# One scan of a state-space step moves behind the gating of the first expert slot

## The reference, cut to what matters

```python
ph   = exp(-(pr*pr + pi*pi)) * exp(1j * arctan2(pi, pr))
conv = ifft(fft(ph**n * pinit) * fft(x))           # along the 32 positions
h    = h + (conv + last * ph**n * ph).real         # the state-space layer
...
top_w, top_i = top_k(xf @ Wg, 2)                   # two of eight experts
y = silu(xf @ W1[e]) * (xf @ W2[e])                # gating: one product
h = h + sum over the two experts of  weight * (y @ W3[e])
```

## Time and profile before

| | |
|---|---|
| median of 3 runs | 538.47 us (538.28 to 539.43) |
| the profiled execution | 540.12 us, of which the span is 538.1 us |
| PE busy | 433.2 us, 81% of the span |
| DVE busy | 303.9 us, 56% |
| ACT busy | 199.4 us, 37% |
| POOL busy | 162.2 us, 30% |
| PE's clock, mean over the span | 0.91 of full speed |

### The profile page before, as it was taken

How to read it: one execution, slowest core, us unless ns; L and a number is a source line. 1 busy time by engine, 2 the same in 40 slices (tenths; PEclk the granted TensorE clock), 3 DMA queues, 4 the chain that set the end, 5 groups by cost and what they waited for, 6 DMA issues and landing times.

```text
span 538.1 us, 9170 instructions
## 1 busy us (share of the span) xinstructions
PE 433.2 (81%) x3291; PEld 282.7 (53%) x3292; DVE 303.9 (56%) x869; ACT 199.4 (37%) x369; POOL 162.2 (30%) x140
## 2 busy tenths in 40 slices
PE   0698798888657754737759999999799999999991
PEld 0254455555554543536525766676565666566561
DVE  0596958784699899998897577726431111111110
ACT  0244545254357513113422662254323233223321
POOL 6041010010020023531042546353254343454422
PEclk9999998979977957855679999999999999999997
DMA  9999010072054100543010422243123226232311
GB/s 179 245 211 204 13 32 3 25 248 84 15 164 179 34 13 2 177 153 132 10 40 11 118 39 41 40 118 50 27 43 49 50 39 185 49 58 39 48 22 19
DMA packets 36102, 43.14 MB, mean 80 GB/s; under 512 B 5216, under 2 KB 30560, under 8 KB 35904
## 3 DMA queue, kind: packets, MB, share of 16 engines
q1 hardware_dynamic: 26384, 32.14, 21.5%
q0 software_dynamic: 7488, 10.23, 12.1%
q10 hardware_dynamic: 2192, 0.27, 0.5%
HBM read 30.96 MB, written 11.53 MB: 79 GB/s over the span
## 4 chain that ended last, share of the span: by engine, by line
PE 57%; DVE 23%; DMA 7%; issue 7%; ACT 3%; SPq 1%; POOL 0%; POOLq 0%; DVEq 0%; ACTq 0%
PE psum L2026 22%; PE psum L2045 11%; PE psum L1723 8%; DMA KT<-in_L_attn_w_o_dram 3%; PE psum L2036 3%; PE psum L1736 2%; PE psum L1748 2%; DMA out_dram<-mixture_rows_out 2%; PE psum L1761 2%; PE psum L2016 1%; DVE st_att L998 1%; DMA KT<-mixture_rows_in,src_i 1%; DVE mx L1032 1%; PE psum L1852 1%; DVE O L1194 1%
## 5 line engine op out<-in xcount | busy, mean ns | idle before, releaser
L1625 DVE TENSOR_TENSOR QT<-QT,psum 128x512 f32<-128x512 f32 x39 | 26.8, 688 | 134.6 <-PE psum L2026 134.4
L1723 PE MATMUL psum<-M2s,M1s 128*128 128x512 f32 x128 | 60.3, 627 | 21.3 <-DMA M1s<-in_L_tok_W_dram 18.8
L2026 PE MATMUL psum<-M1s,KT 128*128 x156 | 75.5, 607 | 1.4 <-ACT KT L789 1.0
L2045 PE MATMUL psum<-M3s,KT 128*128 x312 | 74.2, 381 | 1.5 <-ACT KT L797 0.8
L2026 PE MATMUL psum<-M2s,KT 128*128 x156 | 73.3, 592 | 0.0
L2045 PEld LDWEIGHTS psum<-M3s,KT 128*128 128x128 f32 x312 | 58.5, 190 | 22.0 <-issue 15.9
L808 ACT ACTIVATE O<-psum,gate_slot 128x256 f32<-128x256 f32 x39 | 18.5, 474 | 108.8 <-PE psum L2045 106.0
L502 POOL DMA_INDIRECT KT<-mixture_rows_in,src_i x39 | 41.0, 1052 | 44.2 <-issue 23.3
L1723 PEld LDWEIGHTS psum<-M2s,M1s 128*128 128x128 f32 x128 | 25.1, 201 | 50.6 <-issue 30.0
L2026 PEld LDWEIGHTS psum<-M2s,KT 128*128 128x128 f32 x156 | 29.8, 191 | 37.6 <-issue 37.6
L529 POOL DMA_INDIRECT mixture_rows_out<-O,src_i x17 | 31.6, 1860 | 31.3 <-ACT O L808 12.5
(11 more groups left out here) (398 smaller groups left out, 732.6 us busy)
## 6 DMA issues: line engine op xcount, KB each, us to landing
M3s<-in_x_dram SPq DMA_DIRECT2D x4, 1024.0 KB, 10.6
M3s<-in_L_ffn_W_dram SPq DMA_DIRECT2D x1, 4096.0 KB, 14.3
M2s<-in_L_ffn_W_dram SPq DMA_DIRECT2D x1, 4096.0 KB, 14.8
M1s<-in_L_ffn_W_dram SPq DMA_DIRECT2D x1, 4096.0 KB, 14.0
M3s<-in_x_dram SPq DMA_DIRECT2D x4, 992.0 KB, 14.5
M1s<-vtok SPq DMA_DIRECT2D x64, 34.0 KB, 1.9
mixture_rows_out<-H SPq DMA_DIRECT2D x4, 512.0 KB, 4.2
M1s<-in_L_tok_W_dram SPq DMA_DIRECT2D x2, 512.0 KB, 14.2
```

The lines of the kernel that those rows point to most:

```text
L1625: v.tensor_tensor(sil[:, u, :], sil[:, u, :], bank[3], ALU.mult).then_inc(v_gated, 1)
L1723: last = mm(bank[6 + c], W1s[:, r, P * c:P * (c + 1)], xr[:, i % 2, r].rearrange("p b l -> p (b l)"), start=(n == 0), stop=(n == STRIDE - 1))
L2026: last = mm(z, xrT[:, u, c, :], w[:, bass.ds(e, 1), c, :].rearrange("p a h -> p (a h)"), start=(c == 0), stop=(c == CH - 1))
L2045: last = mm(bank[6][:, 0:DM], actT[:, u, c, :], M3s[:, bass.ds(e, 1), c, :].rearrange("p a d -> p (a d)"), start=(c == 0), stop=(c == HC - 1))
```

## The change

`state_im` is split into the input part `state_im_in` and the scan `state_im_scan`. Step 2 does the input part where it did all of it before, and its scan after the first `slot_gate`, in front of `state_turn(2)`. No instruction is added or removed, and no wait: the steps 0, 1 and 3 call both parts one after the other as before. The wait for DVE's own results in front of the scan moves with it.

```diff
@@ -1106,6 +1106,11 @@
             def state_im(i):
 
+                state_im_in(i)
+                state_im_scan(i)
+
+            def state_im_in(i):
+
                 if i < 2:
                     dve.wait_ge(g_input_im, i + 1)
                 else:
@@ -1113,6 +1118,9 @@
                     dve.wait_ge(v_columns_read, i - 1)
                 for c in range(CH):
                     ln(v.tensor_scalar(cbl(uI)[:, c, :, 0], cbl(uI)[:, c, :, 0], t[19][:, c:c + 1], None, ALU.add))
+
+            def state_im_scan(i):
+
                 own()
                 v.tensor_tensor_scan(uI, RT, uI, 0.0, ALU.mult, ALU.add).then_inc(v_state_im, 1)
@@ -1615,7 +1623,7 @@
             top_expert(3)
             state_re(2)
-            state_im(2)
+            state_im_in(2)
             slot_gates(0, 0, FULL_EARLY, bank[1])
             used_blocks()
@@ -1627,6 +1635,7 @@
             for j in range(FULL):
                 slot_gate(j, j % 2)
                 if j == 0:
+                    state_im_scan(2)
                     state_turn(2)
                 if j == 1:
                     ssm_added(2, SR, [bank[1], bank[7]])
```

## The result

The changed kernel took 542.16 us in the median of 12 runs (539.47 to 543.76), the kernel before 540.00 in the median of 12 beside it. The ratio is 1.0042 (95% interval 1.0026 to 1.0057), so it is 2.3 us slower (1.4 to 3.1). A second comparison, further down, gave 1.0059 (1.0039 to 1.0078). The prediction had the direction. It put the time at 539.8 and its range at 538.6 to 540.7, and the median lies outside that. The loss that it expected was 1.34 us.

A forecast was written before the change was run, and what follows sets the result against it. DVE was taken to bound the kernel up to slot 0's gating, PE behind it. Loss 1.69 us less gain 0.35 gave +1.34, on the median 538.47: 539.8 us, range 538.6 to 540.7.

The forecast's parts named there:

- What bounds, and the hand-over from DVE to PE: At slot 0: DVE sets the time up to the first gating (`slot_gate(0)`), PE behind it.
- Cost 1.69: At PE's state rows of step 2: turned state 1.47 us late, plus 0.22 for a first weight load after a stop.
- Gain 0.46: At slot 0's gating: it starts 0.46 us earlier, as it must still wait for PE's `slot_up(0)`.
- Net +1.23: At slot 0: loss of 1.69 us less gain of 0.46, so `slot_down(0)` ends at 293.09 in place of 291.86.
- cover of 0.92 us: Before the change, step 2's turned state lay ready 0.92 us before PE needed it for the state rows.
- The median's gain of 0.35: At slot 0's gating: gain taken as 0.35 us, since PE's clock may rise later in other executions.
- Does the shift reach the end?: Behind slot 0: neither later PE wait, at 387.84 (2.17 us) or 466.13, swallows the 1.23 us.
- the new stop: On PE before the state rows of step 2: a new wait of 1.47 us for DVE's turned state.
- The third rival: PE's clock falls in its new wait before the state rows: 1.7 to 3.4 us more, 541.5 to 543.2; chance 0.05.
- The sum: Whole kernel: median of the runs shown, 538.47, plus 1.34 gives 539.8 us, 0.25% slower.
- Hidden: PE's waits at 387.84 or 466.13 make up the delay, so the time stays 538.5 us; chance 0.13.
- The gain wins: `slot_up(0)` ends early with the clock high, so the gating gains more than the turn loses: net -0.37, 538.1; chance 0.07.

The follow-up runs named there:

- e10: Kernel before, with the scan of step 2 moved only past the gate weights, still in front of the first gating; ratio 0.9999 to the kernel before.
- e1: Changed kernel, with the state rows of step 2 put behind `slot_down(0)` on PE; ratio 0.9982 to the kernel before.
- e2: Changed kernel, with the turn's first multiply done in DVE's idle time ahead of the first gating; ratio 0.9999 to the kernel before.
- e3: Kernel before, its own scan left in place, with a second scan of the same size added behind the first gating; ratio 1.0052 to the kernel before.
- e6: Changed kernel, with eleven idle matmuls in PE's pause before slot 0; ratio 1.0084 to the kernel before.
- e5: Kernel before, with eleven idle matmuls in PE's pause before slot 0; ratio 1.0045 to the kernel before.
- e16: The changed kernel itself, timed and profiled once more; ratio 1.0059 to the kernel before.
- e17: Kernel before, with a short extra scan (384 elements) between the first gating and the turn; ratio 1.0023 to the kernel before.
- e15: Changed kernel, with three idle matmuls on PE right in front of the state rows of step 2; ratio 1.0044 to the kernel before.
- e18: Changed kernel, with four idle matmuls filling PE's stop before slot 17; ratio 1.0029 to the kernel before.
- e4: Kernel before, with the imaginary scan of step 2 left out and its signal kept; ratio 0.9991 to the kernel before.
- e12: Kernel before, with four idle matmuls in PE's pause before slot 0; ratio 1.0005 to the kernel before.
- e14: Changed kernel, with four idle matmuls before slot 0 and the state rows of step 2 behind `slot_down(0)`; ratio 0.9990 to the kernel before.
- e13: Changed kernel, with four idle matmuls in PE's pause before slot 0; ratio 1.0051 to the kernel before.
- e20: Kernel before, DVE as it was, with PE delayed by three idle matmuls in front of the state rows of step 2; ratio 1.0072 to the kernel before.
- e8: Changed kernel, with eleven idle matmuls before slot 0 and the state rows of step 2 behind `slot_down(0)`; ratio 1.0060 to the kernel before.
- e11: Changed kernel, with one more scan of the same size between the moved scan and the turn; ratio 1.0102 to the kernel before.

## Why the prediction was right and wrong

**What bounds, and the hand-over from DVE to PE.** Right. The change turns on the first gating and `v_ssm_out`, and e10, e1 and e2 undo the loss exactly there.

**The sizes at slot 0.** Right. Cost 1.69, measured 1.68 (e3) and 1.87 (e6 less e5). Gain 0.46, measured 0.43 (e1, b). Net +1.23, measured 1.24 (e16). The cover of 0.92 us was right in size: e17's 0.95 us left a stop of 0.15. But b grew by 0.47 with it, so even so short a stop cost more than its length. The median's gain of 0.35 was a guess between none and 0.46. One profile of the changed kernel has none: the clock rose late, b is 2.52 longer, and of that 0.78 lies ahead of the gating and 1.74 behind it. Those of e15, e16 and e18 have 0.4 to 0.6. So the mean gain can't be told from the 0.35.

**The step of the mechanism that failed** is "Does the shift reach the end?": it has the shift of 1.23 passed on at its own size. It leaned on the sentence that a stop of 2.17 us left the clock at 1.00, for which the sum leaves the clock out. I looked for the fall of the clock at the new stop, where it didn't happen in six profiles, and took the old stop's clock from one execution as a property of the stop. The same stop goes either way. In the seven profiles with the stop unfilled and slot 0 ending where it did or earlier (before, e1, e2, e4, e10, e12, e14) the clock stayed up behind it. In all six in which slot 0 ended 0.5 to 1.7 later, counted from its start (e3, e13, e15, e16, e17, e20), it fell, and c grew by 1.3 to 1.8. It fell in e5, e6 and e8 too, where all of slot 0 began 4.2 to 5.9 us late, and not in e11, where slot 0 ended 5.9 later. e20 changes nothing but PE's lateness and has the fall, in its one profile and by its granted clock in the timed executions; e18 agrees that it is worth about the missing microsecond, within wide intervals. The first profile of the changed kernel is the exception: its b is 2.5 longer, and its clock did not fall. With 1.24 + 1.76 = 3.0 in one profile, 2.5 - 0.2 = 2.3 in the other, the timed 2.3 and 3.2 are covered. The third rival had the mechanism, but the wrong stop, a price of 1.7 to 3.4 where c grew by 1.3 to 1.8, and a chance of 0.05. That the two medians, 542.2 and 543.0, lie in its 541.5 to 543.2 is partly luck, as it too started from the low level below.

The rule of the Trainium skill (TensorE: Matmul & The Clock Gate, "A second HAM failure mode: psum-queue depth-cycling"), that frequent short idle stretches between groups of matmuls can make the clock swing, is borne out in part. In e16 and e20 the clock fell behind a stop of 2.15 and 2.23 us and c grew by 1.76 and 1.31; behind the new stops of about 1.5 us it never fell. How much it matters that such stretches are frequent no run here shows. The prediction set the rule aside on two rows of one execution.

**The level.** The larger part of the miss is no mechanism: it is the first term of "The sum". I put the change on the median of three runs, 538.47, which were a low draw. In the six comparisons the kernel before had medians of 539.4 to 540.0. Of the 2.35 us between 542.16 and 539.81, 1.53 is that, and 0.82 the change. On a level of 540.00 the same forecast would have been 541.3 and its range 540.1 to 542.2, with 542.16 just inside, while the second comparison's loss of 3.2 us would still have been too much for it. The profiled execution, at 540.12, stood nearer to the level than the three.

**The rivals.** "Hidden" fell: e16's b went on to the end and grew. "The gain wins" was not met, since in no profile was the clock up at the start of slot 0 without idle work. What stays open: why the old stop at just these places falls on one side or the other. A shift of 0.5 to 1.7 us did it in six profiles of six, one of 2.5 and one of 5.9 did not, and in e5, e6 and e8, where slot 0 ended 2.3 to 5.8 later counted from PE's last matmuls ahead of its pause, the clock fell again. I have no rule for it from these runs. And how often it falls in the executions that were only timed is inferred from their times and mean clocks, not seen.

## What to carry to other kernels

Before you move work across a hand-over, write down how long before its need each of the two results lies ready: here moving 2.3 us of DVE work bought 0.43 (e1), because PE's own products came next, and cost 1.68 (e3), because its new place had a cover of 0.92. A delay handed to TensorE need not be passed on at its own size: behind a later stop, here one of 2.2 us, the clock may fall, and a shift alone tipped it here, so take the granted clock behind such stops from several executions before you leave it out of a sum. And take the level of a kernel from more than three runs when a quarter of a per cent matters.

## What the hardware showed that I had not expected

At one point of the program TensorE stops for the same transfer in every kernel. Behind 2.15 to 2.25 us the granted clock stayed at 1.00 in eight profiles, and behind 2.15 to 2.23 us it fell to 0.50 within the next products in the six in which slot 0 ended 0.5 to 1.7 us later. The four products behind the stop took 1.98 us in the one case and 2.82 to 3.67 in the other. (In e17, with 2.82, the clock fell later, and the next four took 2.78 in place of 1.88.) Idle matmuls helped only where the work came right behind them: four of them ended 3.6 to 3.7 us before the first products of slot 0, and these ran at 1.2 GHz again, while behind eleven that ended when the rows were there the first four took 1.98. And executions of one and the same kernel lay up to 5.7 us apart (537.86 to 543.53) over the comparisons.
